# The expert stage after a convolutional transformer's main loop, laid out again: four experts at a time, with the weights as the moving operand

## What is computed

```
probs  = softmax(ln(t) @ gate_w.T + gate_b, over tokens)
topv, topi = top_k(probs, 8)               # for each image b and expert e
pooled[b, e] = sum_k topv[b,k,e] * ln(t)[b, topi[b,k,e]]
h[e]   = gelu([pooled[:, e], 1] @ weight1[e])     # 129 x 512 per expert
o[e]   = [h[e], 1] @ weight2[e]                   # 513 x 128 per expert
t[b, topi[b,k,e]] += topv[b,k,e] * o[e][b]        # additions to rows of t
```

## Time and profile before

| | |
|---|---|
| three runs | 2418.95 us median (2418.85 to 2420.6) |
| the profiled execution's own time | 2421.3 us |
| its span in the trace | 2419.6 us |
| TensorE busy, share of the span | 2044.8 us, 85% |
| ScalarE / VectorE / GpSimd busy | 1896.7 / 1888.8 / 1988.7 us |
| memory traffic | read 306.78 MB, written 138.41 MB |
| mean granted clock of TensorE | 0.901 of full speed |

### The profile page before, as it was taken

How to read it: one execution, slowest core, us unless ns; L and a number is a source line. 1 busy time by engine, 2 the same in 40 slices (tenths; PEclk the granted TensorE clock), 3 DMA queues, 4 the chain that set the end, 5 groups by cost and what they waited for, 6 DMA issues and landing times.

```text
span 2419.6 us, 42280 instructions
## 1 busy us (share of the span) xinstructions
PE 2044.8 (85%) x11801; PEld 1470.5 (61%) x11801; DVE 1888.8 (78%) x4793; ACT 1896.7 (78%) x4817; POOL 1988.7 (82%) x2070
## 2 busy tenths in 40 slices
PE   5799999999999999999999999999976556999920
PEld 4666666666666666666666666666632224899920
DVE  3489899999999999999999999999988859311110
ACT  7999999999999999999999999999944331222200
POOL 1199999999999999999999999999999966000087
PEclk9999999999999999999999999999999865555565
DMA  4388888888888888888888888888665541355233
GB/s 153 120 240 219 217 213 232 220 223 213 226 228 221 212 217 228 223 220 218 235 214 222 210 226 225 223 216 233 169 154 140 157 131 43 106 151 155 79 35 34
DMA packets 111054, 447.75 MB, mean 185 GB/s; under 512 B 10573, under 2 KB 52404, under 8 KB 61684
## 3 DMA queue, kind: packets, MB, share of 16 engines
q1 hardware_dynamic: 81140, 302.61, 37.6%
q0 software_dynamic: 29696, 142.61, 32.4%
HBM read 306.78 MB, written 138.41 MB: 184 GB/s over the span
## 4 chain that ended last, share of the span: by engine, by line
POOL 31%; ACT 24%; PE 17%; issue 16%; DVE 10%; DMA 1%; POOLq 0%; SPq 0%; ACTq 0%; DVEq 0%
POOL U L369 11%; ACT U L471 11%; POOL U L374 10%; PE T L663 5%; ACT UT L429 4%; POOL zn L390 3%; ACT zT L435 3%; POOL out_dram L407 3%; PE G L654 2%; PE O L654 2%; ACT LTS L444 2%; PE O L557 2%; PE G L624 2%; ACT LTS L485 2%; POOL U L381 2%
## 5 line engine op out<-in xcount | busy, mean ns | idle before, releaser
L471 ACT ACTIVATE U<-xa,nA,rA 128x128 f32<-128x128 f32 x2048 | 837.2, 481 | 0.6 <-issue 0.6
L369 POOL TENSOR_TENSOR U<-U,bet 128x512 f32<-128x512 f32 x512 | 679.3, 1327 | 0.8
L624 PEld LDWEIGHTS G<-UT 128*128 128x128 f32 x4096 | 536.8, 192 | 228.8 <-issue 224.1
L390 POOL TENSOR_TENSOR zn<-U,rZ 128x512 f32<-128x512 f32 x512 | 585.8, 1144 | 15.2 <-PE T L613 13.2
L374 POOL TENSOR_TENSOR U<-U,rO 128x512 f32<-128x512 f32 x512 | 560.3, 1094 | 9.7 <-ACT rO L453 9.7
L624 PE MATMUL G<-UT 128*128 128x128 f32 x4096 | 542.7, 276 | 0.0
L557 PE MATMUL O<-U,MT 128*128 128x512 f32 x1024 | 528.0, 597 | 0.0
L606 PE MATMUL T<-ident,U 128*128 128x128 f32 x2048 | 323.3, 281 | 128.8 <-ACT UT L429 113.3
L745 DVE BATCH_NORM_STATS2 stA<-xa 128x6 f32<-128x256 f32 x1024 | 385.0, 422 | 59.7 <-DMA xa<-in_x 48.9
L727 DVE BATCH_NORM_STATS2 stO<-O 128x6 f32<-128x256 f32 x1024 | 384.7, 419 | 55.3 <-PE O L557 54.7
L606 PEld LDWEIGHTS T<-ident,U 128*128 128x128 f32 x2048 | 222.6, 142 | 335.3 <-issue 301.3
(11 more groups left out here) (139 smaller groups left out, 2013.2 us busy)
## 6 DMA issues: line engine op xcount, KB each, us to landing
xa<-in_x SPq DMA_DIRECT2D x128, 1024.0 KB, 6.2
U<-in_x POOLq DMA_DIRECT2D x128, 1024.0 KB, 9.0
out_dram<-U SPq DMA_DIRECT2D x128, 1024.0 KB, 7.8
U<-in_L_ffn_weight SPq DMA_DIRECT2D x128, 256.0 KB, 2.9
xa<-out_dram,U POOLq DMA_INDIRECT x64, 2.7
out_dram<-U POOLq DMA_INDIRECT x64, 3.3
U<-in_L_ffn_weight SPq DMA_DIRECT2D x1, 128.0 KB, 2.5
LTS<-in_L_conv_wq SPq DMA_DIRECT2D x1, 64.0 KB
```

The source lines that it names most:

```text
L369: gp.tensor_tensor(rows(a, i), rows(a, i), bet_b, ALU.add).then_inc(S["gb"], 1)
L390: gp.tensor_tensor(zn[:, i % 2, :].rearrange("p (h w) -> p h w", w=W), rows(a, i), rZ[:, k % 2, i % IC * TI:(i % IC + 1) * TI].unsqueeze(2 ...
L471: last = sc.activation(utile(a, i, j), xa[:, k % XR, h * W:(h + 1) * W], ACT.Identity, scale=rA[:, k % 2, h:h + 1], bias=nA[:, k % 2, h:h ...
L624: last = te.matmul(G[:, 0:P], v, v, start=(i == 0 and j == 0), stop=(i == NI - 1 and j == TI - 1))
```

## The change

The stage after the main loop is written anew; the main loop keeps its steps.

- **Layout.** The 128 partitions hold (place 0 to 7, one of 16 experts of a quarter). PE spreads the results of each image over partitions (`spread`, first for images 0 to 14 at step 575, then for the last one), DVE picks and decodes them (`places`, step 577 and after the loop) into `TQ`, `rowf` and `idx` of four quarters q.
- **Order.** Nothing of the expert stage is left between the last image's steps but the first `spread` and `places`. GpSimd fetches after the loop, quarter by quarter, 16 fetches each; only the last fetch of the first quarter waits for the last image's codes.
- **Weights.** The ring has 16 places instead of 8. The first 16 experts' weights are requested once image 14 needs its half of `U` no more; later ones when `layer2` of the group four before is done.
- **Experts in groups of four**, 16 groups in a loop of 23 slots. Each of four experts has 32 output partitions; `PT` (16 columns) is stationary, and the weights move: 512 columns in layer one, 4 x 128 in layer two. The biases are added by matmuls (`biases`). The gelu reads the bank itself. The hidden values are turned by four transposes (`turn1`), the outputs by one (`turn2`).
- **Additions by quarter.** In slots 7 to 22 unit u = 0 to 15 (quarter u // 4, images 4(u % 4) to 4(u % 4) + 3) is turned (`outputs`), weighted, combined and added: four indirect DMAs per unit. A unit waits for the additions of the same images of the quarter before, and no DMA waits for its neighbour.

PE's order in a slot is its loop at the end of its part of the diff; DVE's and ACT's likewise.

The core of the diff (lines removed are those of the listing above: `late`, `gather` and everything after `bodies` in each engine's list):

```diff
--- before
+++ after
...
+            def weights(e):
+                slot = e % EQN
+                if e >= EQN:
+                    sp.wait_ge(R_["o"], (e - EQN) // 4 + 1)
+                sp.dma_start(wring[:, slot:slot + 1, 0:HID], w1v[0:W, e:e + 1, :]).then_inc(s_w[slot // 4], 16)
+                sp.dma_start(wring[:, slot, HID:2 * HID].rearrange("p (a c o) -> p a c o", a=1, c=HC),
+                             w2v[:, e:e + 1, :, :]).then_inc(s_w[slot // 4], 16)
+            sp.wait_ge(S["zn"], (NB - 1) * NI)
+            for k in range(NK):
+                sp.wait_ge(s_store[k], 16 * (NB // 2))
+            for e in range(EQN):
+                weights(e)
...
+            for q in range(Q):
+                for n in range(NB):
+                    if q == 0 and n in (0, NB - 1):
+                        pool.wait_ge(R_["idx"], 1 if n == 0 else 2)
+                        for k in range(2 * NK):
+                            pool.wait_ge(s_store[k], 16 * (NB // 2 - (k >= NK and n == 0)))
+                    gp.indirect_dma_start(out=R[:, q, n, :], out_offset=None, in_=rows_v,
+                                          in_offset=bass.IndirectOffsetOnAxis(ap=idx[:, q, n:n + 1], axis=0),
+                                          ).then_inc(s_rows[q][n // 8], 16)
+            for q in range(Q):
+                for h in range(2):
+                    pool.wait_ge(s_rows[q][h], 128)
+            for u in range(NG):
+                q, g = divmod(u, 4)
+                pool.wait_ge(R_["c"], u + 1)
+                pool.wait_ge(R_["idxs"], u + 1)
+                wait(pool, s_sc[g], 64 * q)
+                for i in range(4):
+                    n = 4 * g + i
+                    gp.indirect_dma_start(out=rows_v,
+                                          out_offset=bass.IndirectOffsetOnAxis(ap=idxs[:, q, n:n + 1], axis=0),
+                                          in_=C[:, g, i * W:(i + 1) * W], in_offset=None,
+                                          bounds_check=NB * P * P - 1, oob_is_err=False,
+                                          compute_op=ALU.add).then_inc(s_sc[g], 16)
...
+            for t in range(SLOTS):
+                if t < NG and t % 4 == 0:
+                    pooled(t // 4)
+                if t < NG:
+                    act.wait_ge(R_["h"], t + 1)
+                    wait(act, R_["trh"], t - 1)
+                    sc.activation(Hs[:, t % 2, :], O[t % 2][:, :], ACT.Gelu).then_inc(R_["ge"], 1)
+                if 0 <= t - 2 < NG:
+                    g = t - 2
+                    act.wait_ge(R_["o"], g + 1)
+                    wait(act, R_["tro"], g - 1)
+                    sc.activation(OUTs[:, g % 2, :], O[2][:, 0:W], ACT.Copy).then_inc(R_["ou"], 1)
+                if t < NG and t % 4 == 2 and t // 4 + 1 < Q:
+                    scales(t // 4 + 1)
+                if 0 <= t - 7 < NG:
+                    u = t - 7
+                    act.wait_ge(R_["cmm"], u + 1)
+                    wait(act, s_sc[u % 4], 64 * (u // 4))
...
+            def pooling(q):
+                pe.wait_ge(R_["fw"], q + 1)
+                wait(pe, R_["p_done"], q)
+                for n in range(NB):
+                    last = te.matmul(T0[:, n * EQN:(n + 1) * EQN], R[:, q, n, :], FW[:, q % 2, n, :], start=True, stop=True)
...
+            def biases(out, g, b):
+                for i in range(4):
+                    te.matmul(out[32 * i:32 * i + 32, :], ident[0:E, 4 * g + i:4 * g + i + 1].to_broadcast([E, 32]), b,
...
+            def layer1(g):
+                q = g // 4
+                if g % 4 == 0:
+                    pe.wait_ge(R_["p_done"], q + 1)
+                wait(pe, R_["ge"], g - 1)
+                biases(O[g % 2], g, b1s)
+                pe.wait_ge(s_w[g % 4], 128 * (q + 1))
+                for i in range(4):
+                    e = 4 * g + i
+                    last = te.matmul(O[g % 2][32 * i:32 * i + NB, :], PT[:, q % 2, e % EQN, :], wring[:, e % EQN, 0:HID],
+                                     start=False, stop=True)
...
+            def turn1(g):
+                pe.wait_ge(R_["ge"], g + 1)
+                wait(pe, R_["ht"], g)
+                for c in range(HC):
+                    last = te.transpose(T1[:, c * P:(c + 1) * P], Hs[:, g % 2, c * P:(c + 1) * P], ident[:, :])
...
+            def layer2(g):
+                pe.wait_ge(R_["ht"], g + 1)
+                wait(pe, R_["ott"], g)
+                biases(O[2][:, 0:W], g, b2s)
+                for c in range(HC):
+                    for i in range(4):
+                        e = (4 * g + i) % EQN
+                        last = te.matmul(O[2][32 * i:32 * i + NB, 0:W], HTs[:, g % 2, c * P + 32 * i:c * P + 32 * i + NB],
+                                         wring[:, e, HID + c * W:HID + (c + 1) * W], start=False, stop=(c == HC - 1))
+                last.then_inc(R_["o"], 1)
...
+            def turn2(g):
+                pe.wait_ge(R_["ou"], g + 1)
+                te.transpose(O[2][:, W:W + P], OUTs[:, g % 2, :], ident[:, :]).then_inc(R_["tro"], 1)
...
+            def codes(u):
+                if u == 0:
+                    pe.wait_ge(R_["codc"], 1)
+                wait(pe, R_["eq"], u)
+                q, g = divmod(u, 4)
+                for i in range(4):
+                    r = q * NB + 4 * g + i
+                    last = te.matmul(G[:, i * P:(i + 1) * P], ident[0:E, r:r + 1].to_broadcast([E, P]), CT, start=True, stop=True)
...
+            def outputs(u):
+                q, g = divmod(u, 4)
+                pe.wait_ge(R_["ott"], 4 * q + 4)
+                wait(pe, R_["v"], u)
+                for i in range(4):
+                    last = te.transpose(LT[:, i * W:(i + 1) * W],
+                                        OT[:, q % 2, 4 * g + i, :], ident[:, :])
...
+            def combine(u):
+                q, g = divmod(u, 4)
+                pe.wait_ge(R_["v"], u + 1)
+                wait(pe, R_["c"], u)
+                for i in range(4):
+                    last = te.matmul(MB[:, i * W:(i + 1) * W], EQ[:, q % 2, 4 * g + i, :], V[:, u % 2, i * W:(i + 1) * W],
+                                     start=True, stop=True)
...
+            for t in range(SLOTS):
+                if t < NG and t % 4 == 0:
+                    pooling(t // 4)
+                if t < NG:
+                    layer1(t)
+                if 0 <= t - 3 < NG:
+                    turn2(t - 3)
+                if 0 <= t - 7 < NG:
+                    outputs(t - 7)
+                if 0 <= t - 1 < NG:
+                    turn1(t - 1)
+                if t < NG:
+                    codes(t)
+                if 0 <= t - 2 < NG:
+                    layer2(t - 2)
+                if 0 <= t - 7 < NG:
+                    combine(t - 7)
...
+            def prepare(q):
+                p = q % 2
+                for h in range(2):
+                    dve.wait_ge(s_rows[q][h], 128)
+                    for m in range(4):
+                        n = 8 * h + 2 * m
+                        last = ve.bn_stats(stR[:, p, n:n + 2, :].rearrange("p n s -> p (n s)"),
+                                           R[:, q, n:n + 2, :].rearrange("p h w -> p w h"))
+                last.then_inc(R_["rbn"], 1)
+                dve.wait_ge(R_["rbn"], q + 1)
+                wait(dve, R_["rln"], q - 1)
+                ve.tensor_scalar(vR[:, p, :], stR[:, p, :, 2], 1.0 / W, EPS_T, ALU.mult, ALU.add).then_inc(R_["rvar"], 1)
+                ve.tensor_tensor(R[:, q, :, :], R[:, q, :, :], stR[:, p, :, 1].unsqueeze(2).to_broadcast([P, NB, W]),
+                                 ALU.subtract).then_inc(R_["cen"], 1)
+                dve.wait_ge(R_["rr"], q + 1)
+                ve.tensor_tensor(wvb[:, p, :], TQ[:, q, :, 0], rR[:, p, :], ALU.mult).then_inc(R_["wv"], 1)
...
+            def equal(u):
+                q, g = divmod(u, 4)
+                f = slice(4 * g, 4 * g + 4)
+                dve.wait_ge(R_["row"], u + 1)
+                wait(dve, R_["cmm"], u - 7)
+                ve.tensor_tensor(EQ[:, q % 2, f, :], G[:, :].rearrange("p (j w) -> p j w", j=4),
...
+            for t in range(SLOTS):
+                if 0 <= t - 3 < NG:
+                    g = t - 3
+                    q = g // 4
+                    dve.wait_ge(R_["tro"], g + 1)
+                    wait(dve, R_["xt"], 4 * (q - 1))
+                    h = 4 * (g % 4)
+                    ve.tensor_copy(OT[:, q % 2, :, :].rearrange("p n (k e) -> p n k e", e=EQN)[:, :, :, h:h + 4],
+                                   O[2][:, W:W + P].rearrange("p (e n) -> p n e", n=32)[:, 0:NB, :].unsqueeze(2)
+                                   .to_broadcast([P, NB, K, 4])).then_inc(R_["ott"], 1)
+                if 0 <= t - 7 < NG:
+                    u = t - 7
+                    q, g = divmod(u, 4)
+                    dve.wait_ge(R_["xt"], u + 1)
+                    wait(dve, R_["cmm"], u - 1)
```

(78 more changed lines are left out.)

365 lines of the change are left out of this document (139 added, 226 removed).

## The result

The changed kernel takes 2222.35 us median (2218.71 to 2226.05, four runs) beside 2419.77 (2418.85 to 2424.44, four runs) of the kernel before on the same chip: 0.918 of the time, 95% interval 0.9161 to 0.92. The profiled execution took 2223.25 us, its span is 2221.5, the mean granted clock 0.957. The forecast was 2216 (2185 to 2280), faster.

A forecast was written before the change was run, and what follows sets the result against it. The old end was bound by DVE, PE and GpSimd in turn. First expert 2000.6, slot 4 at 2033, twelve slots of 10.5 to 2159, then 52.2 + 2.6 + 3.3: span 2217, median 2216, range 2185 to 2280.

The forecast's parts named there:

- The three stretches: Old end of some 460 us: pooling on DVE, then experts on PE at half clock, then additions on GpSimd alone.
- The overlap: Expert layers: matmuls to four groups of 32 output partitions run all at once, 8 records in 2 steps.
- The rival with the draining of PE between tilings: PE stays at 1.2 GHz (chance 0.27); about six tiling changes a slot drain PE, 0.16 us each: 2251.
- the forecast case: The main case, chance 0.35: both clock levels by turns, slots 4 to 15 about 10.5 us, median 2216.
- That makes slots 4 to 15 about 10.5 us: bandwidth's 10.0, with fills: Expert slots 4 to 15: DMA of weights and additions, 10.0 us a slot, sets their length, about 10.5 each.
- binds less than bandwidth: Expert slots: weights' latency, 9 to 11 us from request to landing, spans two slots and matters less than DMA bandwidth.
- PE's own list: PE's work per slot: 8.3 us at half, 4.2 at full clock; with combining, from slot 7, 10.9 and 5.5.
- The clock stayed at 1.2 GHz: Rival for the expert slots, chance 0.27: PE stays at half clock throughout, 2235, or 2251 with handoffs.
- Weights and additions don't disturb each other: Denies the rival, chance 0.12, that additions hold weights up: 14 us for each of slots 4 to 15, 2259.
- no overlap: Slower rival in `layer1` and `layer2`, chance 0.04: groups don't overlap and the clock stays half, 2501.
- the change not doing what it says: Rival, chance 0.02: experts wait for the last fetches or additions for the last expert; about 2278 or more.
- Its own signs of being wrong: Layer-one groups over 3 us; slots' chain through DVE or ACT; additions over 2 us each; main loop over 5 us longer.

The follow-up runs named there:

- no_pack: Changed kernel with all expert matmuls at the full 128 output columns, so no groups run side by side: 2355.18 us, ratio 0.9722.
- both_spread: Changed kernel with earlier layer-one weight requests, split statistics, and fetches of the last two quarters spread over slots: 2201.54 us, ratio 0.9091.
- again: The changed kernel once more, nothing edited, on chip B: 2260.19 us, ratio 0.9354.
- again2: The changed kernel unchanged, on chip C beside `spread2`: 2223.77 us.
- spread2: Second run of the `spread` kernel, on chip C beside the unchanged changed kernel: 2219.97 us.
- no_reload: Changed kernel loading only the first 16 experts' weights, which all four quarters use: 2262.12 us.
- early_w1: Changed kernel with layer-one weights requested once layer one of the group four before is done, two slots earlier: 2260.67 us.
- split_prep: Changed kernel with the next quarter's statistics in slots 0 and 1 of a quarter instead of slot 2: 2264.48 us.
- both: Changed kernel with the edits of `early_w1` and `split_prep` together: 2247.21 us.
- spread: Changed kernel with the fetches of quarters 2 and 3 issued by four, each after layer one of a further group: 2224.47 us.
- no_adds: Changed kernel without the 64 additions to the output: 2222.32 us.
- late_start: Changed kernel with DVE waiting for the last quarter's fetches before `prepare(0)`: 2286.8 us, ratio 0.9439.

## Why the prediction was right, and where it was not

**Mechanism.** The three stretches were read rightly, and so was what the change makes of them: the selection out of the queue, the first quarter alone, additions under the experts. The overlap, on which everything hung, was taken from two groups of 64 and holds for four of 32 (1.05 us for eight records, 3.70 without it). The figure of the Trainium skill (TensorE: Matmul & The Clock Gate, measured speedup table: 2.38 for three column tiles) would, as an estimate, have added a quarter to each packed step. Here two packed steps take 0.98 us at full clock, from the first start to that of the next group. Of this 0.10 is a change of tile shape (next paragraph), which leaves 0.44 a step; eight full-width records of `no_pack` take 3.54, 0.44 each. So the overlap costs nothing that can be seen.

The rival with the draining of PE between tilings came in part. Eight records of `combine` at full clock take 0.89 us where their neighbours on both sides have the same shape (`no_pack`, first two lines), and 1.09 where both differ (`both_spread`, last two):

```profile
2145.76 1.06 PE L745 MATMUL MB<-U 128*128 128x128 f32 x8
2146.65 3.64 PE L676 MATMUL T<-U,xa 128*128 128x16 f32 x32
...
2091.05 1.16 PE L759 MATMUL MB<-U 128*128 128x128 f32 x8
2092.14 1.06 PE L695 MATMUL O<-U,ident 64*32 64x512 f32 x8
```

Where one side differs it is 0.99, in both kernels. So a change of shape between two groups (128 or 64 rows, full or packed columns) costs 0.10 us here, less than the 0.16 of the rival. A slot with `combine` has seven, 0.7 us, and the forecast case had them at nothing.

**The sum**, term by term:

| term | forecast | measured |
|---|---|---|
| last logits there | 1966.4 + 2.3 | 1973.0 |
| to the last codes | 12.7 + 4.2 = 16.9 | 16.6 |
| fetch, `prepare(0)`, pooling and copy | 2.7 + 4.9 + 7.4 | 2.7, 4.4, 7.7 |
| first expert | 2000.6 | 2004.5 |
| layer one of slot 4 (`biases`) | 2033 | 2038.8 |
| slots 4 to 15, each | 10.5 | 9.7 |
| unit 9 of the additions starts | 2161.6 | 2163.1 |
| its seven units | 52.2 | 52.1 |
| behind them | 3.3 | 6.3 |
| span | 2217 | 2221.5 |

Three terms were mis-sized. *`places`* was put at 4.5 us, half of it covered: +2.3. It takes 6.0, and the last logits come 6.6 us later than in the kernel before (1973.0 against 1966.4), of which 2.2 had come before `places` began. DVE's timeline in the changed kernel shows two operations of 60 elements at five times what the forecast gave them; GpSimd's own of the same time stand below:

```profile
1941.62 0.64 DVE L803 TENSOR_TENSOR hot<-G,mask 128x480 f32<-128x480 f32 x1
...
1944.54 1.03 DVE L818 TENSOR_SCALAR wT<-wT 128x60 uint32<-128x60 uint32 x1
...
1946.09 1.07 DVE L824 TENSOR_TENSOR Gs<-wT 128x60 f32<-128x60 uint32 x1
1947.19 0.22 DVE L827 TENSOR_TENSOR UT<-Gs,boff 128x60 f32<-128x60 f32 x1
...
1944.43 1.09 POOL L382 TENSOR_TENSOR zn<-U,rZ 128x512 f32<-128x512 f32 x1 [0.37 <-PE T L648]
...
1946.04 1.04 POOL L382 TENSOR_TENSOR zn<-U,rZ 128x512 f32<-128x512 f32 x1 [0.52 <-PE T L648]
```

Each of the two starts within 0.11 us after such an operation of GpSimd and ends 0.05 to 0.07 us after it. The other runs show the same with other lines of `places` (L827 in `again`, L816 and L827 in `again2`): the small operation that starts just behind GpSimd's, by up to 0.20 us, lasts until that one has ended. Nine further runs agree, and `spread2`, where none falls there, has none that long; the reductions (L807) are not held. So `places` pays for standing beside GpSimd's part of the main loop, which its price, taken where no such operation ran, left out.

*The end* was put at 3.3 us, an addition's landing: the landing is that (2213.4 to 2216.7), but the sync engine and GpSimd then close the program for another 4.8. The trace of before had it: its last addition was issued at 2412.8 of a span of 2419.6. *The slots*: 9.7 us instead of 10.5, nearly right by a wrong reason. Layer one of slot 4 came 5.8 us late and the shorter slots took most of that back, so that 2216 lies within 7 us of 2222 is in part luck.

**The step that failed** is "That makes slots 4 to 15 about 10.5 us: bandwidth's 10.0, with fills", with its neighbour that the latency of the weights "binds less than bandwidth". `no_reload` takes three quarters of the DMA share away and gains nothing; `early_w1` and `split_prep` together shorten the slots to 8.0 us (`both`), although the same weights have to come in them. What fills a slot is PE, at a clock of 0.8 to 0.86, plus two waits: the weights' latency (8.5 us of PE's time in all) and DVE's `prepare`, 5.6 us from the first statistics to the copy behind them in each of three quarters (6.4 us of PE's time in all), which the forecast had only in DVE's sum and not as a stall of PE. PE's own list was undersized too. `both_spread` shows it without waits: `biases` (L695 there) in its chain at full clock, every 6.63 us where the forecast had 5.5,

```profile
2085.58 0.99 PE O L695 x8
...
2092.21 0.99 PE O L695 x8
...
2098.84 3.49 PE T L689 x32
```

and `spread` at half clock before the combining begins, layer one (L697 there) every 9.4 us where the forecast had 8.3:

```profile
2046.04 1.91 PE L697 MATMUL O<-U 128*16 128x512 f32 x8
...
2055.42 1.91 PE L697 MATMUL O<-U 128*16 128x512 f32 x8
```

Of the 1.1 us that each list is over its forecast, the seven changes of shape are 0.7 at full clock (before the combining begins there are six, 0.6 if they cost the same at half clock, an estimate). The rest is in the records, such as 0.44 instead of 0.43 for 512 columns. In the changed kernel's window from 2040 to 2150 PE is busy 94 of 110 us, so 8.3 of a slot's 9.7 are PE's and 1.4 its waits. Once the waits are gone, slots 8 to 11 do run with DMA near 1.0, as the forecast said, but at 8.4 us and not at 10.

**Additions.** They were to start near 2065 and did at 2076.8: `V` of the first unit stands on DVE behind `prepare(2)` (until 2070.8). That is the same stall. They run gapless from 2147.8, not 2160, so GpSimd rules the last nine units, not seven. The two errors cancel in the table, since unit 9 comes at nearly the same time.

**Rivals.** The clock stayed at 1.2 GHz only until 2030; later windows have both levels, 0.83 in the mean. Weights and additions don't disturb each other so that it could be seen (`no_adds`: slots no shorter). The end rivals, no overlap and the change not doing what it says, are out; `no_pack`, which is the first of them, comes to 0.972 and not above 1: the rival took half clock for it, and the run had 0.96 in its slots.

**Its own signs of being wrong.** Two of the four that the forecast named are in the trace: the chain in the slots goes through DVE, three times, and the main loop ends over 5 us later (6.6 at the last logits). The other two aren't: eight layer-one records take 1.05 or 1.91 us, and an addition 1.58.

**What no part of the forecast held**: the stretch. With it the same kernel takes 2260, within the range but for a reason outside the argument.

## What to carry to other kernels

Work that ends in a fixed train of indirect additions is timed by when that train starts and how many pauses it has; count those two before anything else, and move whatever stands before its first unit. Where an engine has several waits in a slot, removing one may bring nothing that can be told: read busy time and clock together, and remove the waits together. Price an operation in the surroundings in which it will stand: beside another engine's work, or between matmuls of another tile shape, it costs more than in a quiet stretch. A cure is only shown beside a control on the same chip that has the fault: compare variants only with the unchanged kernel of the same session.

## What was not expected of the hardware

- Four groups of 32 output partitions in float32 run entirely side by side: 8 records of 512 columns in 1.05 us (full clock) and 1.91 (half), against 3.70 at full width. A change of tile shape between groups of matmuls costs 0.10 us (0.89, 0.99 and 1.09 us for the same eight records with none, one and two).
- A small DVE operation of 60 elements that starts just behind a GpSimd operation of 1.04 to 1.10 us lasts until that one has ended, 0.91 to 1.08 us instead of about 0.2.
- The stretch: on two of three chips, PE, ACT and DVE stand nearly still for 38 us while GpSimd issues indirect fetches back to back, every 1.25 us; PE issues a record every 1.4 to 2.8 us in it, and ACT is released 38 us after the matmuls it waits for. It didn't come where the experts start after the fetches (`late_start`, one kernel). On a third chip, and in the first runs, the same program has none. What does this, whether it belongs to the chip or to the moment (A and B had one session each), and whether issuing the fetches by fours avoids it, is open: the one chip on which that was tried has no stretch to avoid.
- With the later weights left out PE is busy 93 instead of 89 of 100 us, at 0.79 instead of 0.86, and gets no more done. Why the clock is lower in that trace is open.
